# Expert tiles for half of the feed-forward chunks of a fused feed-forward, attention, feed-forward kernel

## Chip, cores and metric

One core of a Trainium2 chip. The metric is the device time of one execution in microseconds (us); the program is timed in several runs, and one more execution is recorded by the hardware profiler.

## The reference

x is 16 sequences of 256 tokens with 128 features, 4096 tokens in all, in float32. Three residual steps follow each other:

```
x = x + 0.5 * ffn(layernorm(x))
x = x + attention(layernorm(x))        # 16 heads of 64, causal
x = x + 0.5 * ffn(layernorm(x))        # the same weights
```

The feed-forward has 64 routed experts (128 to 64 to 128, SiLU gate) and one shared expert:

```
scores = sigmoid(x @ gate_w.T);  sc = scores + gate_bias
group_scores = top_k(sc in 8 groups of 8, 2).sum;   keep the best 4 groups
tidx = top_k(masked sc, 8);   tw = 2.5 * scores[tidx] / sum(scores[tidx])
y = sum over experts e:  w_dense[:, e] * ((silu(x @ wg[e]) * (x @ wu[e])) @ wd[e])
y = y + (silu(x @ sg) * (x @ su)) @ sd
```

Only 8 of the 64 weights w_dense[:, e] of a token are not zero.

## The kernel before

Tokens are cut into 8 chunks of 512 (CT = 4 tiles of 128). Both feed-forwards are one function, `ffn` (L382 on), with attention (L936 on) between them, each in a block of its own.

**Dense slots.** A chunk passes 33 slots: 32 pairs of experts, which fill the 128 rows of TensorE together, and the shared expert alone. In slot q TensorE computes gate and up of pair q (`up`, L491) and the down product of pair q - 3 (`down`, L510). Every token is multiplied with every expert. Gate and up weights, and the normalised tokens xT, are split in a high and a low float32r part, and `three` (L485 to L489) forms each product from three matmuls:

```
nc.tensor.matmul(bank[:, :], hi, rhs_hi, start=start, stop=False)                 # L487
nc.tensor.matmul(bank[:, :], lo, rhs_hi, start=False, stop=False)                 # L488
return nc.tensor.matmul(bank[:, :], hi, rhs_lo, start=False, stop=stop)           # L489
```

The down product (L521) is one float32 matmul of 512 columns into the bank `acc`, over all 33 slots of the chunk. ScalarE turns the gate into `hid` by SiLU (L592), VectorE multiplies it with up (`gated_product`, L648) and with the routing weights (`weighted_product`, L659). TensorE reports gate_done, up_done and down_done, one update each per slot. `hid` has three buffers (HIDS).

**Routing weights.** VectorE works out the mix of the next chunk in 25 route steps (`route`, two per slot from slot 14); TensorE turns it, ScalarE copies it to mixT, SyncE stores it to `mix_rows` in HBM (L363) and reads it back, spread over the partitions, as `mix_wide` (L789, L792): 8 groups of four slots per chunk, two transfers of 512 KB each, double-buffered.

**Turning.** A chunk also has transposes of the normalised tokens (L164), of the logits (L177), of the mix (L184) and of y (L528), and three matmuls for the logits (L170).

**Attention.** 64 steps, one for four heads of one sequence: q, k and v projections from split weights (L1024 to L1026, L1042 to L1044), scores (L1059) with the mask (L1063), 12 transposes of the probabilities (L1080), values (L1099), output (L1116). ScalarE does the exponentials (L1188, L1191), copies k (L1201) and the turned probabilities (L1210). VectorE copies q (L1255), v (L1263) and o (L1284), normalises (L1270, L1275) and takes the maxima (L1292, L1293). During its last steps the first chunk of the second feed-forward is routed.

GpSimd computes only constants and 1/sqrt of the variances (L348, L353). The order on each engine is written out by hand in its block; the loops over chunks run in `Fori` loops.

## Time and profile before

| | us |
|---|---|
| median of 3 runs (lowest, highest) | 1830.7 (1830.08, 1833.13) |
| the profiled execution | 1831.43 |
| its span, first to last instruction | 1829.7 |
| TensorE matmuls busy | 1781.7 (97%) |
| TensorE weight loads busy (beside the matmuls) | 1255.0 (69%) |
| VectorE busy | 1331.9 (73%) |
| ScalarE busy | 774.6 (42%) |
| GpSimd busy | 36.6 (2%) |

PE is TensorE's matmuls, PEld its weight loads, DVE is VectorE, ACT ScalarE, POOL GpSimd, SP SyncE; PEq, SPq are their instruction queues. Durations of matmuls overlap, since they are pipelined, so distances between starts say more than durations. A bracket at the end of a row tells how long the engine had been idle before it and what released it. The DMA share is that of the core's 16 DMA engines.

### The profile page before, as it was taken

To read this page: it belongs to the slowest core of one execution; us is meant where nothing else is said; L and a number is where in the kernel's file an instruction comes from. 1 tells how busy PE (TensorE), PEld (TensorE's weight loads), DVE (VectorE), ACT (ScalarE), POOL (GpSimd) and SP (SyncE) were. 2 spreads that over 40 slices of the span, in tenths; PEclk is the share of its full clock that TensorE was granted. 3 is DMA by queue.
4 is the path that set the end of the run, shared out by engine and by line. 5 is a ranking of instruction groups with operands and counts; after the bars stand their busy time and mean duration, and the time that the engine had idled before them with its cause. 6 is when DMAs were issued, how large, how long until landed. Compare 5 with 4: busy or idle time off the path is not lost.

```text
span 1829.7 us, 30208 instructions
## 1 busy us (share of the span) xinstructions
PE 1781.7 (97%) x9049; PEld 1255.0 (69%) x9049; DVE 1331.9 (73%) x3327; ACT 774.6 (42%) x1971; POOL 36.6 (2%) x84
## 2 busy tenths in 40 slices
PE   5899999999999999999999999879999999999999
PEld 3566666666666667777778777756666666666665
DVE  5777677676776678888888888767677676777765
ACT  3333323233232256767666666633323233232322
POOL 0000000000000000000000000000000000000000
PEclk8999999999999999999999999999999999999999
DMA  9954554455545500000000000034554455544553
GB/s 206 173 122 110 115 117 105 107 115 115 117 100 109 116 1 2 0 0 0 0 0 0 0 0 0 1 82 109 120 118 108 107 122 121 117 104 111 120 124 75
DMA packets 109530, 149.60 MB, mean 82 GB/s; under 512 B 30128, under 2 KB 43056, under 8 KB 109488
## 3 DMA queue, kind: packets, MB, share of 16 engines
q1 hardware_dynamic: 109488, 149.08, 36.9%
q8 instruction: 21, 0.34, 0.1%
q14 instruction: 21, 0.17, 0.0%
HBM read 144.87 MB, written 4.19 MB: 81 GB/s over the span
## 4 chain that ended last, share of the span: by engine, by line
PE 61%; DVE 2%; DMA 0%; issue 0%; ACT 0%; SPq 0%; POOLq 0%; POOL 0%; DVEq 0%
PE banks L521 12%; PE banks L489 7%; PE banks L487 7%; PE banks L488 7%; PE banks L1059 6%; PE banks L1099 5%; PE banks L1080 4%; PE banks L1116 3%; PE banks L1024 2%; PE banks L1063 2%; PE banks L1025 2%; PE banks L1026 2%; PE banks L1043 1%; PE banks L1044 1%; PE banks L1042 1%; DMA f_mix_wide<-mix_rows 0%
## 5 line engine op out<-in xcount | busy, mean ns | idle before, releaser
L592 ACT ACTIVATE f_hid<-banks 128x512 f32<-128x512 f32 x528 | 315.4, 597 | 835.9 <-PE banks L521 831.5
L648 DVE TENSOR_TENSOR f_hid<-banks,f_hid 128x512 f32<-128x512 f32 x528 | 363.9, 690 | 338.0 <-ACT f_hid L592 336.3
L521 PE MATMUL banks<-f_hid,wd 128*128 128x512 f32 x1056 | 540.7, 594 | 10.7 <-DVE f_hid L659 10.6
L487 PE MATMUL banks<-r_xT_hi,wg_hi 128*128 (+1 forms) x528 | 393.0, 744 | 2.4 <-PEq L951 2.4
L659 DVE TENSOR_TENSOR f_hid<-f_mix_wide,f_hid 128x512 f32<-128x512 f32 x512 | 352.9, 690 | 38.4 <-DMA f_mix_wide<-mix_rows 24.3
L521 PEld LDWEIGHTS banks<-f_hid,wd 128*128 128x128 f32 x1056 | 196.8, 188 | 67.6 <-DVE f_hid L659 13.1
L487 PE MATMUL banks<-r_xT_hi,wu_hi 128*128 (+1 forms) x528 | 209.9, 398 | 0.0
L489 PE MATMUL banks<-r_xT_lo,wu_hi 128*128 (+1 forms) x528 | 209.9, 398 | 0.0
L488 PE MATMUL banks<-r_xT_hi,wu_lo 128*128 (+1 forms) x528 | 208.8, 396 | 0.0
L489 PE MATMUL banks<-r_xT_lo,wg_hi 128*128 (+1 forms) x528 | 208.3, 394 | 0.0
L488 PE MATMUL banks<-r_xT_hi,wg_lo 128*128 (+1 forms) x528 | 207.3, 393 | 0.0
L487 PEld LDWEIGHTS banks<-r_xT_hi,wg_hi 128*128 128x128 f32 x528 | 100.6, 190 | 111.2 <-issue 110.2
L488 PEld LDWEIGHTS banks<-r_xT_hi,wg_lo 128*128 128x128 f32 x528 | 100.9, 191 | 108.2 <-issue 107.3
L1210 ACT COPY a_probT<-banks 128x512 f32<-128x512 f32 x192 | 106.3, 587 | 147.7 <-PE banks L1080 147.7
L1275 DVE TENSOR_SCALAR a_prob<-a_prob,a_inv 128x128 f32<-128x128 f32 (+1 forms) x512 | 129.0, 316 | 4.5
L1191 ACT ACTIVATE a_prob<-banks,a_bias 128x256 f32<-128x256 f32 x256 | 123.6, 483 | 0.0
L1059 PE MATMUL banks<-a_kT,a_qT 64*128 64x128 f32 (+1 forms) x1024 | 118.5, 350 | 0.3 <-issue 0.2
L489 PEld LDWEIGHTS banks<-r_xT_lo,wu_hi 128*128 128x128 f32 x528 | 99.2, 188 | 24.7
L489 PEld LDWEIGHTS banks<-r_xT_lo,wg_hi 128*128 128x128 f32 x528 | 99.6, 189 | 22.5
L487 PEld LDWEIGHTS banks<-r_xT_hi,wu_hi 128*128 128x128 f32 x528 | 99.6, 189 | 22.4 <-issue 0.4
L488 PEld LDWEIGHTS banks<-r_xT_hi,wu_lo 128*128 128x128 f32 x528 | 99.5, 188 | 22.6
L1080 PE MATMUL banks<-ident,a_prob 128*128 128x128 f32 x768 | 106.4, 275 | 1.1 <-DVE a_prob L1275 1.0
(153 smaller groups left out, 2155.4 us busy)
## 6 DMA issues: line engine op xcount, KB each, us to landing
f_mix_wide<-mix_rows SPq DMA_DIRECT2D x252, 512.0 KB, 6.5
landing<-in_L_ffn_We_gate SPq DMA_DIRECT2D x4, 512.0 KB, 7.1
landing<-in_L_ffn_We_up SPq DMA_DIRECT2D x4, 512.0 KB, 7.8
wd<-in_L_ffn_We_down SPq DMA_DIRECT2D x4, 512.0 KB, 6.8
mix_rows<-r_mixT SPq DMA_DIRECT2D x32, 64.0 KB, 2.1
out<-x_all SPq DMA_DIRECT2D x8, 256.0 KB, 6.7
f_mix_wide<-mix_rows SPq DMA_DIRECT2D x4, 384.0 KB, 5.4
f_mix_wide<-mix_rows SPq DMA_DIRECT2D x4, 128.0 KB, 3.0
```

Of the source, the lines that this page charges most:

```text
L487: nc.tensor.matmul(bank[:, :], hi, rhs_hi, start=start, stop=False)
L488: nc.tensor.matmul(bank[:, :], lo, rhs_hi, start=False, stop=False)
L489: return nc.tensor.matmul(bank[:, :], hi, rhs_lo, start=False, stop=stop)
L521: nc.tensor.matmul(acc[:, :], w["wd"][:, p * P:(p + 1) * P], hid[:, p % HIDS, :], start=(p == 0), stop=(p == PAIRS)).then_inc(down_done, 1)
L592: nc.scalar.activation(hid[:, p % HIDS, :], gate_bank[p % 3][:, :], ACT.Silu).then_inc(silu_done, 1)
L648: nc.vector.tensor_tensor(hid[:, p % HIDS, :], up_bank[p % 3][:, :], hid[:, p % HIDS, :], ALU.mult)\
L659: nc.vector.tensor_tensor(hid[:, p % HIDS, :], mix_wide[:, g % 2, p % SPREAD, :], hid[:, p % HIDS, :], ALU.mult).then_inc(weighted, 1)
L1059: nc.tensor.matmul(scores[pair][h][:, cols], qT[side_rows, i, pair, rows_q], kT[side_rows, i, pair, cols_k], start=(cols.start == 0), stop ...
L1080: mm = nc.tensor.transpose(bank[:, j * P:(j + 1) * P], prob[:, n * P:(n + 1) * P], w["ident"][:, :])
L1191: e = nc.scalar.activation(prob[:, o + P:o + NPB], scores[pair][h][:, P:NPB], ACT.Exp, bias=bias[:, i, pair, 1, h:h + 1], scale=HD ** -0.5 ...
L1210: nc.scalar.copy(probT[:, g * 4 * P:(g + 1) * 4 * P], turn_bank[g][:, :]).then_inc(probT_done, 1)
L1275: m = nc.vector.tensor_scalar(prob[:, a:b], prob[:, a:b], inv[:, i, pair, late, h:h + 1], None, ALU.mult)
```

## The change

Of the 8 chunks of each feed-forward four stay dense (0 to 3 in the first, 4 to 7 in the second) and four become sparse.

**Sparse chunks.** Their tokens are routed to a list: VectorE marks the eight experts of each token, counts per expert and lays the 16,384 (token, expert) rows out by expert, each expert's share rounded up to whole tiles of 128 rows (`plan`, `place`). GpSimd writes the normalised tokens by 128 indirect transfers, 128 rows of 512 bytes each, to `x_rows` in HBM (`dispatch`). The rows fill at most 191 tiles, taken by fours in QUADS_R = 48 **quads**; four more quads carry the shared expert. A quad: SyncE loads 4 tiles (256 KB), TensorE turns them, multiplies them with gate and up of the expert of each tile, turns the hidden rows, multiplies them with down; ScalarE and VectorE copy between, and SyncE stores 256 KB to `y_rows`. Which expert a tile belongs to is read at run time into registers of TensorE (`load_experts`). Four pipeline stages of successive quads stand in one step. Then GpSimd fetches the eight result rows of each token (`gather`, 128 more indirect transfers) and VectorE adds them with their weights (`add`), for the first feed-forward during attention (4 per step), for the second one between dense slots (8 per five slots, from slot 39). Before the first scatter `x_rows` (12.6 MB) is cleared by 12 transfers of 1 MB from ScalarE's queue, one every third slot from slot 16 (`clear_rows`). The first scatter begins at slot 57 of 132, the second in attention step 49 with 60 of its 128 transfers; the other 68 follow in the second feed-forward, whose quads stand behind its first dense chunk.

**Dense slots.** Gate, up and down are one float32 matmul each; the split weights and their making are gone. Only the up product reports (`pair_done`), and the down product once per chunk (`chunk_done`); `hid` has four buffers. VectorE takes three route steps per slot.

**Attention.** Fully written out. The copies of q and v move to ScalarE, the output product behind the v projection, and the sparse chunks of the second feed-forward and its first dense one are normalised and routed here.

The diff replaces most of the file; its core (line numbers are of the new file):

```diff
@@ dense slot, TensorE (L764 on)
-            def up(c, p):
...
-                if p >= 3 or not first:
-                    pe.wait_ge(silu_done, SLOTS * c + p - 2)
...
-                three(g, "wg", p, xh, xl).then_inc(gate_done, 1)
-                if p >= 3 or not first:
-                    pe.wait_ge(gated, SLOTS * c + p - 2)
...
-                three(u, "wu", p, xh, xl).then_inc(up_done, 1)
...
-            def down(c, p):
-                if p == PAIRS:
-                    pe.wait_ge(gated, SLOTS * (c + 1))
-                else:
-                    pe.wait_ge(weighted, PAIRS * c + p + 1)
...
-                nc.tensor.matmul(acc[:, :], w["wd"][:, p * P:(p + 1) * P], hid[:, p % HIDS, :],
-                                 start=(p == 0), stop=(p == PAIRS)).then_inc(down_done, 1)
+        def up(g):
+            c, p = divmod(g, SLOTS)
+            x = d.xT[:, c % 2, :]
...
+            experts = slice(2 * p, 2 * p + rows // F)
+            if g >= 3:
+                pe.wait_ge(silu_done, g - 2)
...
+            nc.tensor.matmul(gate_bank[g % 3][0:rows, :], w["gu"][:, 0, experts, :].rearrange("p e f -> p (e f)"), x,
+                             start=True, stop=True)
+            if g >= 3:
+                pe.wait_ge(gated, g - 2)
+            nc.tensor.matmul(up_bank[g % 3][0:rows, :], w["gu"][:, 1, experts, :].rearrange("p e f -> p (e f)"), x,
+                             start=True, stop=True).then_inc(pair_done, 1)
...
+        def down(g):
+            c, p = divmod(g, SLOTS)
+            if p == PAIRS:
+                pe.wait_ge(gated, g + 1)
+            else:
+                pe.wait_ge(weighted, PAIRS * c + p + 1)
...
+            rows = F if p == PAIRS else P
+            mm = nc.tensor.matmul(acc[:, :], w["wd"][0:rows, 2 * p, :], d.hid[0:rows, g % HIDS, :],
+                                  start=(p == 0), stop=(p == PAIRS))
+            if p == PAIRS:
+                mm.then_inc(chunk_done, 1)
@@ quads, TensorE (L561 on)
+        def load_experts(j):
+            if j < SPARSE:
+                expert[j] = [E] * CT
+                return
+            i = j - SPARSE
+            if i == 0:
+                pe.wait_ge(r.plan_step, PLAN_STEPS - 1)
+            _, expert[j] = nc.values_load_multi_w_load_instructions(
+                b.ids[i:i + 1, :], engines=PE_ONLY, min_val=0, max_val=E,
+                skip_runtime_bounds_check_because="the number of 64 experts that end at or before a tile")
...
+        def gate_up(j):
+            load_experts(j)
+            e = expert[j]
+            pe.wait_ge(xT_copied, j + 1)
+            if j >= 2:
+                pe.wait_ge(hid_done, j - 1)
+            for t in range(CT):
+                wt = w["gu"][:, :, e[t], :] if j < SPARSE else \
+                    w["gu"][:, :, bass.ds(e[t], 1), :].rearrange("p k a f -> p k (a f)")
+                mm = nc.tensor.matmul(B[j % 2][:, t * P:(t + 1) * P], q.xqT[:, j % 2, t * P:(t + 1) * P], wt,
+                                      start=True, stop=True)
+            mm.then_inc(gu_done, 1)
...
+        def step(j):
+            if ok(j):
+                turn(j)
+            if ok(j - 1):
+                gate_up(j - 1)
+            if ok(j - 2):
+                turn_hid(j - 2)
+            if ok(j - 3):
+                down(j - 3)
@@ quads, SyncE (L692 on)
+        def load(i):
+            if i == 0:
+                sp.wait_ge(r.scattered, 16 * TOPK * CT * SPARSE)
+            if i >= 3:
+                sp.wait_ge(turned, SPARSE + i - 2)
+            sp.dma_start(q.xq[:, i % 3, :, :], rows(x_rows, i)).then_inc(loaded[i % 3], 16)
+        def store(i):
+            sp.wait_ge(y_read, SPARSE + i + 1)
+            sp.dma_start(rows(y_rows, i), q.yq[:, i % YBUFS, :, :]).then_inc(y_stored[i % YBUFS], 16)
@@ GpSimd
+        def dispatch(i):
+            tile, half = divmod(i, 2)
+            k, t = divmod(tile, CT)
+            if t == 0 and half == 0:
+                pool.wait_ge(idx_done, k + 1)
+            for j in HALVES[half]:
+                nc.gpsimd.indirect_dma_start(
+                    x_rows[:, :], bass.IndirectOffsetOnAxis(ap=b.idx[:, f, CT * k + t, j:j + 1], axis=0),
+                    b.xk[:, k, t, :], None).then_inc(scattered, 16)
...
+        def gather(t, js=range(TOPK)):
+            if t >= GBUFS and js[0] == 0:
+                pool.wait_ge(added, added_before + TOPK * (t - GBUFS + 1))
+            for j in js:
+                nc.gpsimd.indirect_dma_start(
+                    g_buf[:, t % GBUFS, j, :], None, y_rows[:, :],
+                    bass.IndirectOffsetOnAxis(ap=b.idx[:, f, t, j:j + 1], axis=0)).then_inc(gathered[t % GBUFS], 16)
@@ the added rows, VectorE
+                nc.vector.scalar_tensor_tensor(x, g_buf[:, t % GBUFS, j, :], b.w8[:, f, t, j:j + 1], x,
+                                               ALU.mult, ALU.add).then_inc(added, 1)
@@ attention, ScalarE (L1346 on)
+            def slot(c, k, last):
+                soft = k >= 1 and (k - 1 < STEPS or not last)
+                if soft:
+                    exps(c, k - 1)
+                if k < STEPS or not last:
+                    copy_q(c, k)
+                    copy_k(c, k)
+                if k % QUADS == 1 and k >= LEAD_A:
+                    copy_y(c, k)
+                if soft:
+                    copy_probT(c, k - 1)
+                if k < STEPS or not last:
+                    copy_v(c, k)
```

On TensorE's queue a dense slot in the middle of a chunk of the first feed-forward was this (f_hid are the hidden rows, r_xT the normalised tokens):

```order
L487 MATMUL banks<-r_xT_hi,wg_hi 128x512 [waits f1_silu_done]
L488 MATMUL banks<-r_xT_hi,wg_lo 128x512
L489 MATMUL banks<-r_xT_lo,wg_hi 128x512
L487 MATMUL banks<-r_xT_hi,wu_hi 128x512 [waits f1_gated]
L488 MATMUL banks<-r_xT_hi,wu_lo 128x512
L489 MATMUL banks<-r_xT_lo,wu_hi 128x512
L521 MATMUL banks<-f_hid,wd 128x512 [waits f1_weighted]
```

and a slot of the changed kernel, followed by the next slot and a routed quad step (f1q_xq the loaded rows, f1q_hidT the turned hidden rows, r_ids the expert numbers), are these on the same queue:

```order
L778 MATMUL banks<-r_xT_d,gu 128x512 [waits f1d_silu_done]
L782 MATMUL banks<-r_xT_d,gu 128x512 [waits f1d_gated]
L794 MATMUL banks<-f1_hid,wd 128x512 [waits f1d_weighted]
```

```order
L556 MATMUL banks<-ident,f1q_xq 128x128 [waits f1q_xT_copied,f1q_loaded1]
L556 MATMUL banks<-ident,f1q_xq 128x128 x3
L568 TENSOR_LOAD r_ids
L581 ISA [waits f1q_hid_done,f1q_xT_copied]
L581 MATMUL banks<-gu,f1q_xqT 128x128
L581 ISA
L581 MATMUL banks<-gu,f1q_xqT 128x128
L581 ISA
L581 MATMUL banks<-gu,f1q_xqT 128x128
L581 ISA
L581 MATMUL banks<-gu,f1q_xqT 128x128
L591 MATMUL banks<-ident,f1q_hidq 128x128 [waits f1q_hT_odd_copied,f1q_hT_even_copied,f1q_hid_done]
```

Seven matmuls became three. In the quad step two transposes of hidden rows and four down products, each behind its own address instruction, follow the last row; the register load stands between the transposes and the gate products.

On ScalarE's queue an attention step of the changed kernel runs from the q copy to the v copy like this (L1312 and L1320 stood on VectorE's):

```order
L1312 COPY a_qT<-banks 128x512 [waits a_proj_done,a_scores_done]
L1328 COPY a_kT<-banks 128x512 [waits a_proj_done,a_scores_done]
L1337 COPY a_probT<-banks 128x512 [waits a_o_done,a_prob_turned]
L1337 COPY a_probT<-banks 128x512 [waits a_prob_turned] x2
L1320 COPY a_v<-banks 128x512 [waits a_proj_done,a_o_done]
```

The v copy stands behind the last copy of the turned probabilities, and the next step's exponentials behind it.

## Rows read from the trace of the kernel before

**Rows 1.** Busy time by stretch: us, busy us (x instructions), clock, DMA share, GB/s
```profile
0.00:652.80 652.80, 624.55 (x2259) 416.91 (x2259) 450.58 (x999) 209.04 (x338) 13.65 (x38) 0.99 0.55 121
652.80:1211.90 559.10, 545.08 (x4555) 427.97 (x4555) 456.50 (x1408) 373.18 (x1318) 14.55 (x32) 0.99 0.00 0
1211.90:1829.70 617.80, 612.12 (x2235) 410.09 (x2235) 424.84 (x920) 192.38 (x315) 8.44 (x14) 1.00 0.51 114
```
**Rows 2.** Timeline of TensorE, one dense slot: start us, us, engine line
```profile
400.76 0.79 PE L487 MATMUL banks<-r_xT_hi,wg_hi 128*128 x1
401.39 0.39 PE L488 MATMUL banks<-r_xT_hi,wg_lo 128*128 x1
401.61 0.39 PE L489 MATMUL banks<-r_xT_lo,wg_hi 128*128 x1
...
403.00 0.79 PE L487 MATMUL banks<-r_xT_hi,wg_hi 128*128 x1
```
**Rows 3.** Timeline, the last four down products
```profile
1821.28 3.62 PE L521 MATMUL banks<-f_hid,wd 128*128 128x512 f32 x8
```
**Rows 4.** Timeline, turning of y in two successive chunks
```profile
1298.93 0.60 PE L528 MATMUL banks<-ident,r_yT 128*128 128x128 f32 x4
...
1375.57 0.60 PE L528 MATMUL banks<-ident,r_yT 128*128 128x128 f32 x4
```
**Rows 5.** Timeline of TensorE and its weight loads, parts of one attention step
```profile
802.54 0.74 PEld L1116 LDWEIGHTS banks<-a_oT,po 128*128 128x128 f32 x4
...
802.66 1.02 PE L1116 MATMUL banks<-a_oT,po 128*128 128x256 f32 x4
...
803.64 0.28 PE L1043 MATMUL banks<-pv_lo,n_xT_hi 128*128 128x256 f32 x1
803.75 0.28 PE L1044 MATMUL banks<-pv_hi,n_xT_lo 128*128 128x256 f32 x1
...
805.84 1.04 PE L1080 MATMUL banks<-ident,a_prob 128*128 128x128 f32 x8
806.81 0.93 PE L1059 MATMUL banks<-a_kT,a_qT 64*128 64x128 f32 x8
...
807.99 1.52 PE L1099 MATMUL banks<-a_probT,a_v 128*64 128x256 f32 x16
```
**Rows 6.** Busy time in two stretches of the first feed-forward, columns as in rows 1
```profile
10.00:20.00 10.00, 8.31 (x23) 6.30 (x24) 7.07 (x21) 6.07 (x8) 0.00 (x0) 1.00 1.28 226
...
300.00:400.00 100.00, 100.00 (x366) 67.26 (x365) 73.44 (x178) 30.83 (x52) 1.21 (x2) 1.00 0.51 112
```
**Rows 7.** The page's DMA issues, the mix store: count, size, us to landing
```profile
mix_rows<-r_mixT SPq DMA_DIRECT2D x32, 64.0 KB, 2.1
```
**Rows 8.** Timeline of ScalarE, two copies of turned probabilities
```profile
806.48 1.07 ACT L1210 COPY a_probT<-banks 128x512 f32<-128x512 f32 x2 [1.03 <-PE banks L1080]
```
**Rows 9.** Timeline, first matmuls of attention and of the second feed-forward
```profile
652.84 0.35 PE L1024 MATMUL banks<-n_xT_hi,pq_hi 128*128 128x256 f32 x1 [1.05 <-PEq L399]
...
1211.94 0.47 PE L487 MATMUL banks<-r_xT_hi,wg_hi 128*128 128x512 f32 x1 [2.36 <-PEq L951]
```
**Rows 10.** Waits of ScalarE in 700 to 1100: total us, times, longest
```profile
ACT a_probT L1210 <- PE banks L1080: 109.2, 95, 1.4
```
**Rows 11.** Waits of VectorE in 0 to 110: total us, times, longest
```profile
DVE f_hid L659 <- DMA f_mix_wide<-mix_rows: 19.5, 5, 6.4
```
**Rows 12.** Timeline of VectorE in a routed dense slot
```profile
401.00 0.68 DVE L659 TENSOR_TENSOR f_hid<-f_mix_wide,f_hid 128x512 f32<-128x512 f32 x1
...
401.60 0.42 DVE L325 TENSOR_TENSOR r_chosen<-r_chosen,r_score 128x256 f32<-128x256 f32 x1
...
402.05 0.69 DVE L648 TENSOR_TENSOR f_hid<-banks,f_hid 128x512 f32<-128x512 f32 x1
```
**Rows 13.** Timeline of SyncE's queue at the start, two issues
```profile
1.32 0.59 SPq L830 DMA_DIRECT2D f_gw_raw<-in_L_ffn_gate_w  x1
...
3.05 2.37 SPq L810 DMA_DIRECT2D landing<-in_L_ffn_We_up  x1
```
**Rows 14.** Timeline of GpSimd, one layer norm
```profile
1151.48 1.01 POOL L353 TENSOR_TENSOR r_rstd<-r_veps,minus_half 128x4 f32<-128x4 f32 x1
```

More of the change, by code:

```diff
@@ L36 @@
 NG = 8
+TOPK = 8
 TOPK_GROUPS = 4
@@ new lines, with routes_of @@
+TILES = (TOPK * SPARSE * CHUNK - E) // P + E
+QUADS_R = -(-TILES // CT)
+ROWS = QUADS_R * CHUNK
+QUADS_ALL = SPARSE + QUADS_R
+PAD = E // 2
+YBUFS, STORE_LAG, GBUFS = 3, 6, 3
+HALVES = (range(0, TOPK // 2), range(TOPK // 2, TOPK))
+DENSE_STEPS = 25
+SPARSE_STEPS = 23
+PLAN_STEPS = 12
+PLACE_STEPS = 4
+W_STEPS = 3
+WEIGH_STEPS = W_STEPS * CT + 5
+@dataclass(frozen=True)
+class Route:
+    n: int
+    front: int
+    chunk: int
+    dense: int
+    sparse: int
+def routes_of(kinds, by_row=0):
+    out, d, s = [], 0, 0
+    for n, (chunk, is_dense) in enumerate(kinds):
+        out.append(Route(n, n - by_row, chunk, d if is_dense else -1, -1 if is_dense else s))
+        d, s = d + is_dense, s + (not is_dense)
+    return out
@@ L931, in row_norm, with attention @@
     return parts
-def attention(nc, w, x_all, banks, psum, rows, ahead):
+A_ROUTE, A_COUNT, A_PLAN, A_RANK, A_DISPATCH = 14, 44, 45, 48, 49
+A_HEAD, A_MIX = 47, 55
+ADD_LAG = 3
+def attention(nc, w, x_all, banks, psum, rows, b, mix_rows, y_rows, first, second, gathered, added):
     TB = SEQ // P
@@ L942, in attention @@
     QUADS = H // 4
-    STEPS = 2 * QUADS
+    STEPS = NB * QUADS
+    PER_CHUNK = CHUNK // SEQ
+    FRONTS = [4 * n for n in range(SPARSE * PER_CHUNK)] + [32, 37]
+    chunk_of = [q.chunk for q in FIRST if q.sparse >= 0]
+    later, head = [q for q in SECOND if q.sparse >= 0], SECOND[SPARSE]
     NPB = P + SEQ
@@ L1111, in output @@
                         pe.wait_ge(x_updated, b)
-                    if not (last and k == QUADS):
+                    if b + 1 < NB:
                         pe.wait_ge(xT_lo_done, b + 2)
@@ L1159, in slot @@
                     turn_prob(c, k - 1, 2, live)
-                if k % QUADS == 1 and not last:
+                if k % QUADS == 1 and k // QUADS + 1 < NB:
                     turn_xn(c, k)
@@ L1351, in _ @@
+            for k in range(STEPS):
+                if k < 2 * SPARSE * CT:
+                    gather(k // 2, HALVES[k % 2])
+                if k >= A_DISPATCH:
+                    dispatch(k - A_DISPATCH)
+                if front_row(k, 6) is not None:
+                    front_rstd(front_row(k, 6))
+                if moments_row(k) is not None:
+                    rstd_of(moments_row(k))
         @block.sync
         def _(sp):
-            ahead.on_sync(sp)(0)
+            second.on_sync(sp, mix_rows)(head)
@@ L1390, in macaron @@
+        gathered = [ctx.enter_context(nc.semaphore(f"gathered{i}")) for i in range(GBUFS)]
+        added = ctx.enter_context(nc.semaphore("added"))
         banks = ctx.enter_context(nc.psum_tensor("banks", [P, 8 * 512], F32))
         psum = [banks[:, i * 512:(i + 1) * 512] for i in range(8)]
-        b = router_buffers(ctx, nc)
-        first, second = (router(ctx, nc, tag, w, x_all, mix_rows, b) for tag in ("r1_", "r2_"))
-        rows = row_norm(ctx, nc, w, x_all)
-        ffn(nc, "f1_", w, x_all, psum, mix_rows, b, first, rows=rows, load=(x_v, dr))
```

1829 lines of the change are left out of this document (1181 added, 648 removed).

## The prediction

> **What bounds the kernel now.** I read the busy time by stretch first, for the stages and their clock; then TensorE in time order inside a stage; then the other engines and the queues at the same places. The kernel has three stages, first feed-forward, attention, second feed-forward, of 652.8, 559.1 and 617.8 us [rows 1]. TensorE is at work in nearly all of each, at a granted clock of 0.99 to 1.00, which is the 2.4 GHz level. VectorE has 451, 456 and 425 us of work in them, ScalarE at most 373. So TensorE's work sets the time, and what an edit is worth is how much of that work it takes out or adds, plus any new wait that ends last.
>
> One slot of a feed-forward (two experts for 512 tokens) lasts 2.24 us: the first gate product starts at 400.76 and the next slot's at 403.00 [rows 2]. Six split products stand some 0.23 us apart (401.39 and 401.61 are two of them); the down product, one full-precision matmul made of two records, takes the rest, about 0.85 us. The records' own durations overlap, so I go by starts. The four down products at the end confirm the size: 8 records in 3.62 us, 0.45 each with the tail [rows 3]. A whole chunk lasts 76.64 us from one turning of y to the next [rows 4]: 33 slots of 2.24, and 2.7 us for turning, logits and mix.
>
> **Dense slots.** Four of the eight chunks of each feed-forward keep the slots, so 528 become 264. The slot itself changes: the split weights are gone, and gate, up and down are each one full-precision product of 512 columns. Three times 0.85 is 2.55, three times 0.9 is 2.7; I take 2.58, near the back-to-back starts. A dense slot thus gets longer by 0.34 us. Removed 528 x 2.24 = 1183 us, put in 264 x 2.58 = 681 us: -502. Of the 14 routed chunks inside the feed-forwards 10 are left, 4 x 2.7 = -11. That gate and up now report once together, and down only once per chunk, I cost at nothing: ScalarE starts SiLU 0.85 us later, but the down product comes three slots after, and a fourth hid buffer covers the reuse.
>
> **Quads.** Each feed-forward gets 52 steps (4 with the shared expert, 48 of four sorted tiles). One step on TensorE is 4 transposes, 4 gate/up products of 128 columns, 2 transposes and 4 down products. A transpose takes 0.12 us by its neighbours' starts (8 of them from 805.84 to 806.81), and it too is one weight load and 128 columns [rows 5]. A full-precision product is two such halves. The output product of attention has four halves of 256 columns in the 0.86 us from 802.66 to the start of the split product before 803.64, 0.215 each, so 128 columns stream in 0.107, under the 0.12. That gives (4 + 2 + 2 x 4 + 2 x 4) x 0.12 = 2.64, say 2.7 us. The step also loads four expert numbers into registers on TensorE's queue, and then computes each address. The trace has no such load. Below it costs nothing: a loop branch and register work stand in every chunk now and TensorE is at work in all 100 us of a stretch [rows 6], so its queue runs ahead. Above, it costs a memory round trip of 2.1 us, as the 64 KB mix store takes [rows 7], less the 0.5 us of transposes queued ahead. I take 0.3, near the low end, because the down products and transposes of the same step stand ahead of the load and need nothing late. So 3.0 us a step (2.7 to 4.3), and 104 x 3.0 = +312. The Trainium skill (DMA: Bandwidth & Descriptors, Latency and other measured facts) gives a register load a floor of about 600 ns. By that and a queue that does not run ahead at all a step would be 2.8 to 3.3 us and the sum -21 to +31 us from mine; no run here shows it yet.
>
> The other engines fit in a step. ScalarE has about 1.3 us (two 512-column copies take 1.07 together [rows 8], here one and two smaller), VectorE 1.5 us. SyncE moves 256 KB in and 256 KB out; at the 226 GB/s seen while weights in 256 and 512 byte pieces came in [rows 6] that is 2.3 us, so DMA is close behind and comes next if TensorE is faster than I think.
>
> **Joins.** Dense drains, quads fill, the last y rows must land before the gathers: a new block restarts TensorE's queue in 1.05 and 2.36 us today [rows 9], and the quads' pipeline of four steps fills and empties once; I take 12 us per feed-forward, +24 (12 to 40).
>
> **Attention.** The q and v copies leave VectorE for ScalarE. ScalarE now waits 109 us for transposes in 400 us, 2.3 us a step of 8.3 [rows 10], and takes 1.1 more. But the v copy comes after the last probT copy, which ends at 807.55 [rows 8]; the values product behind it starts at 807.99 today [rows 5] and needs the v copy, so it moves to about 808.2: 0.2 us x 64 = +13 (0 to 37). TensorE gets ten more turnings, logits, counts and ranks: +9. VectorE receives 128 weighted additions of 128 columns and the routing, about 2.6 us in a full step (4 x 0.3 and 4 x 0.35, from 0.45 for 256 columns [rows 12]). The two copies that left, 0.69 each by rows of their size [rows 12], give 1.4, and VectorE is idle in (559 - 456) / 64 = 1.6 us of a step [rows 1]: it fits, with little to spare. Sum +22 (5 to 60).
>
> **First chunks.** The clears of the row buffer add 12.6 MB to mix tiles that already made VectorE wait 19.5 us in the first 110 us [rows 11]; +10 (0 to 35). In routed slots VectorE has two 0.60 products and three 0.45 route steps [rows 12], 2.55 of 2.58 us, and LayerNorm spills over: +6 (0 to 20).
>
> **Sum.** 1829.7 - 502 - 11 + 312 + 24 + 22 + 10 + 6 = 1690.7, and 1.7 us outside the span (the profiled execution took 1831.4, the median is 1830.7): **1692 us**.
>
> **GpSimd.** It issues 128 indirect transfers per scatter or gather, 512 in all, 128 rows each. No row shows one. SyncE's plain issues take 0.6 us, those into full rings up to 2.4, GpSimd's own power on four columns 1.01 [rows 13, 14]; I take 1.3 us, and for that T all are hidden: the first scatter has some 229 us (slot 57 to the end of the first quads, T up to 1.8), the second has 68 transfers left in about 99 us (1.46), a gather of 8 has five slots, 12.9 us (1.6), an attention step takes 4 (2.1).
>
> **Rivals.**
> - GpSimd becomes the bound, slower than before. The excess is 128(T - 1.8) + 68(T - 1.46) + 128(T - 1.6); it reaches 139 us, and the present time, at T = 2.07; at 2.1 the kernel takes 1838. For it: VectorE's weighted product reads two SBUF tiles and runs 0.68 of every 2.58 us [rows 12], and if an issue has to wait out one, 1.3 becomes 2.0. Against it the trace has nothing, since GpSimd hardly works in it; and the operations of that kind fill a quarter of a slot. The Trainium skill (SBUF - State Buffer, SBUF: two separate sides) states such a lock between a VectorE operation with two SBUF inputs and a GpSimd operation that reads SBUF; no run here shows it. 10%.
> - Loads do not overlap products: each of the 22 halves costs the 0.19 us of a load record (4 in 0.74 [rows 5]) and not 0.12, a step 4.5 us, 1848 us (2%). Split products of 256 columns 0.12 us apart, each with its load [rows 5], speak against it. Or the register load is wholly exposed, 1827 us (5%).
> - DMA sets the step: 512 KB at half the seen rate is 4.7 us, 1869 us. 3%.
> - It goes better than that: queue ahead of everything, quads 2.7, v copy and clears free: 1692 - 31 - 13 - 16 = 1632. 10%.
> - My case, 70%, 1640 to 1760.
>
> **The numbers.** What a measurement can tell from no change is 0.2%, 3.7 us. Faster has my case, the good one and half of the exposed load, 83%; same the other half, 2%; slower the three that remain, 15%. The range takes the good case in and reaches up to 1.1 us more per quad step: 1630 to 1805.
>
> **What would show it.** Right: starts of gate products 2.58 us apart; quad transposes 3.0 us apart; attention steps some 0.3 us longer than now; first indirect gathers 1.3 us apart on GpSimd, and no wait for scattered rows ahead of the first routed quad. Wrong: TensorE idle behind its own queue in each quad step; VectorE waiting on gathered rows; a second stage over 600 us; slots of the first chunk stretched by mix tiles for much over 20 us.

## The result and the profile after

The changed kernel takes **2058.2 us** (median of 4 runs, 2055.3 to 2061.2) against 1831.9 for the one before: 1.124 times as long (95% interval 1.121 to 1.126). Forecast were 1692 us, and a range up to 1805. The page of the changed kernel (busy us, share of the span, instructions; then tenths in 40 slices):

```profile
span 2053.6 us, 26930 instructions
PE 1659.6 (81%) x8683; PEld 1054.5 (51%) x8683; DVE 1197.8 (58%) x3446; ACT 779.5 (38%) x2105; POOL 549.6 (27%) x607
PE   5899792399999777777678997639738999898899
POOL 1000657600000433323230002360570000646430
PEclk9999995699999888888889998869969999999899
```

TensorE has 1660 us of work and stands for 394. It was at work in nearly all of each stage before [rows 1]. The slices in which it falls (the fifth, seventh and eighth, the 14th to 21st, the 25th to 27th, the 29th and 30th) are slices in which GpSimd is at work. Stretches of it, cut by time, say the same more finely. Columns: TensorE, weight loads, VectorE, ScalarE, GpSimd (busy us, instructions), granted clock, DMA share, GB/s.

```profile
208.00:412.00 204.00, 115.89 (x249) 48.29 (x248) 83.66 (x210) 29.37 (x47) 129.48 (x130) 0.77 0.33 87
275.00:300.00 25.00, 25.00 (x69) 11.77 (x68) 21.38 (x48) 9.26 (x13) 19.31 (x20) 1.00 0.51 129
300.00:325.00 25.00, 12.39 (x22) 4.27 (x20) 6.38 (x25) 1.22 (x3) 19.21 (x20) 0.69 0.36 95
325.00:350.00 25.00, 4.99 (x6) 1.80 (x6) 5.38 (x12) 1.17 (x2) 19.20 (x20) 0.57 0.28 76
1350.00:1375.00 25.00, 0.00 (x0) 0.00 (x0) 0.52 (x2) 1.72 (x8) 18.90 (x21) 0.51 0.16 52
```

From 275 to 300 us all is well beside 20 indirect transfers of GpSimd. From 300 on the transfers go on at the same pace and the three compute engines all but stop, with no engine busy in their place and the DMA engines two thirds idle. From 1350 to 1375, in attention, which needs no data from memory but the gathers, already done by then, TensorE executes nothing at all. What ends it shows in the timelines (start us, us, engine, line, what; in brackets the idle time before and what ended it). ScalarE, then VectorE, then TensorE:

```profile
310.21 0.60 ACT L822 ACTIVATE f_hid<-banks 128x512 f32<-128x512 f32 x1 [9.41 <-remote]
324.98 0.60 ACT L822 ACTIVATE f_hid<-banks 128x512 f32<-128x512 f32 x1 [14.17 <-remote]
341.77 0.60 ACT L822 ACTIVATE f_hid<-banks 128x512 f32<-128x512 f32 x1 [16.19 <-remote]
357.87 0.60 ACT L822 ACTIVATE f_hid<-banks 128x512 f32<-128x512 f32 x1 [15.50 <-remote]
```
```profile
325.60 0.69 DVE L844 TENSOR_TENSOR f_hid<-banks,f_hid 128x512 f32<-128x512 f32 x1 [11.00 <-issue]
```
```profile
301.22 1.02 PE L778 MATMUL banks<-r_xT_d,gu 128*128 128x512 f32 x2
302.08 1.02 PE L782 MATMUL banks<-r_xT_d,gu 128*128 128x512 f32 x2
302.94 1.02 PE L794 MATMUL banks<-f_hid,wd 128*128 128x512 f32 x2
303.80 1.02 PE L778 MATMUL banks<-r_xT_d,gu 128*128 128x512 f32 x2
304.65 1.02 PE L782 MATMUL banks<-r_xT_d,gu 128*128 128x512 f32 x2
...
310.86 2.07 PE L778 MATMUL banks<-r_xT_d,gu 128*128 128x512 f32 x2 [4.33 <-ACT f_hid L822]
312.73 1.92 PE L782 MATMUL banks<-r_xT_d,gu 128*128 128x512 f32 x2
...
325.62 2.08 PE L778 MATMUL banks<-r_xT_d,gu 128*128 128x512 f32 x2 [8.38 <-issue]
```

A SiLU (L822) waits for one thing, the semaphore that the up product (L782) raises, and TensorE may be three slots ahead of it. The slot that starts at 310.86 needs the SiLU of three slots before, at 310.21; so the SiLU at 324.98 belongs to the slot of 301.22, that at 341.77 to 303.80, that at 357.87 to 310.86. Their up products ended at 303.1, 305.7 and 314.6 (the profile models a matmul's end, but the down product started no more than 0.5 us behind each of them): the updates were seen **22, 36 and 43 us late**, one of them about every 16 us. "remote" is the profile's word for a releaser that it cannot name: the update came long after its matmul. In the other directions nothing is late. VectorE (325.60) starts as ScalarE ends, and TensorE (325.62) beside it. The hold in attention is of the same kind: VectorE waits for TensorE's values product, and goes on 2 us after the last transfer of that run.

```profile
1375.60 0.96 POOL L467 DMA_INDIRECT x_rows<-r_xk,r_idx  x1 [0.31 <-issue]
```
```profile
1378.95 0.69 DVE L1447 COPY a_oT<-banks 128x512 f32<-128x512 f32 x1 [28.40 <-remote]
1381.82 0.59 ACT L1312 COPY a_qT<-banks 128x512 f32<-128x512 f32 x1 [29.52 <-PE banks L1164]
```

The waits, summed, put it in one list (who waited for whom, us in all, times, longest). The long ones of ScalarE and VectorE end with TensorE's updates or an unnamed releaser; those of TensorE follow from them:

```profile
ACT f_hid L822 <- remote: 196.1, 20, 16.2
DVE f_hid L844 <- issue: 178.7, 32, 21.0
PE banks L1162 <- DVE a_oT L1447: 161.8, 40, 31.2
DVE a_oT L1447 <- remote: 102.2, 10, 28.4
ACT a_qT L1312 <- remote: 51.0, 9, 9.9
DVE f_hid L857 <- DMA f_mix_wide<-mix_rows: 26.4, 5, 8.8
```

The waits of ScalarE and VectorE that end with an unnamed releaser are none in the kernel before and 428 us in 63 waits in the changed one. The experiments use this sum as the sign of the hold.

### The profile page after: what moved, and what is told of

It is laid out like the page before. It is cut to its first block and busy times, and to the rows that moved or that the text cites. A ratio compares the mean times of both kernels' runs of the same rounds, so it can differ in the third digit from the quotient of the medians.

```text
span 2053.6 us, 26930 instructions
## 1 busy us (share of the span) xinstructions
PE 1659.6 (81%) x8683; PEld 1054.5 (51%) x8683; DVE 1197.8 (58%) x3446; ACT 779.5 (38%) x2105; POOL 549.6 (27%) x607
## 3 DMA queue, kind: packets, MB, share of 16 engines
q0 software_dynamic: 16384, 33.59, 5.9%
## 5 line engine op out<-in xcount | busy, mean ns | idle before, releaser
L822 ACT ACTIVATE f_hid<-banks 128x512 f32<-128x512 f32 (+1 forms) x264 | 156.8, 597 | 683.1 <-PE banks L782 432.5
L844 DVE TENSOR_TENSOR f_hid<-banks,f_hid 128x512 f32<-128x512 f32 (+1 forms) x264 | 181.7, 688 | 352.6 <-issue 178.7
L778 PE MATMUL banks<-r_xT_d,gu 128*128 128x512 f32 x528 | 293.1, 638 | 114.6 <-issue 86.3
L467 POOL DMA_INDIRECT x_rows<-r_xk,r_idx x256 | 252.3, 985 | 189.5 <-issue 79.5
L794 PE MATMUL banks<-f_hid,wd 128*128 128x512 f32 x528 | 282.3, 619 | 22.4 <-DVE f_hid L857 11.4
L782 PE MATMUL banks<-r_xT_d,gu 128*128 128x512 f32 x528 | 286.7, 626 | 0.0
L778 PEld LDWEIGHTS banks<-r_xT_d,gu 128*128 128x128 f32 x528 | 100.1, 201 | 241.2 <-issue 202.5
L857 DVE TENSOR_TENSOR f_hid<-f_mix_wide,f_hid 128x512 f32<-128x512 f32 x256 | 175.6, 686 | 28.9 <-DMA f_mix_wide<-mix_rows 26.4
L501 POOL DMA_INDIRECT f_g<-y_rows,r_idx x128 | 128.2, 1002 | 209.4 <-DMA y_rows<-f2q_yq 132.3
L782 PEld LDWEIGHTS banks<-r_xT_d,gu 128*128 128x128 f32 x528 | 105.5, 200 | 139.1 <-issue 133.1
L501 POOL DMA_INDIRECT a_g<-y_rows,r_idx x128 | 124.7, 975 | 141.4 <-POOLq L1582 104.5
L1299 ACT ACTIVATE a_prob<-banks,a_bias 128x128 f32<-128x128 f32 x256 | 98.3, 384 | 75.5 <-DVE a_bias L1459 59.1
```

The source lines that it names most:

```text
L467: nc.gpsimd.indirect_dma_start(x_rows[:, :], bass.IndirectOffsetOnAxis(ap=b.idx[:, f, CT * k + t, j:j + 1], axis=0), b.xk[:, k, t, :], Non ...
L501: nc.gpsimd.indirect_dma_start(g_buf[:, t % GBUFS, j, :], None, y_rows[:, :], bass.IndirectOffsetOnAxis(ap=b.idx[:, f, t, j:j + 1], axis=0 ...
L778: nc.tensor.matmul(gate_bank[g % 3][0:rows, :], w["gu"][:, 0, experts, :].rearrange("p e f -> p (e f)"), x, start=True, stop=True)
L782: nc.tensor.matmul(up_bank[g % 3][0:rows, :], w["gu"][:, 1, experts, :].rearrange("p e f -> p (e f)"), x, start=True, stop=True).then_inc( ...
L794: mm = nc.tensor.matmul(acc[:, :], w["wd"][0:rows, 2 * p, :], d.hid[0:rows, g % HIDS, :], start=(p == 0), stop=(p == PAIRS))
L822: nc.scalar.activation(d.hid[0:rows, g % HIDS, :], gate_bank[g % 3][0:rows, :], ACT.Silu)\
```

## Experiments

**Theory A**: while GpSimd issues transfers back to back, TensorE's semaphore updates reach their waiters late. **Theory B**: the other terms of my sum were too low (quads, clears, a fuller attention step). Every time below stands beside 1830 to 1833 us for the kernel before. e7, e9, e11 and e14 are medians of four executions, the others are single ones; those of one kernel lay up to 14 us apart (e7), in the others within 6.

**1. No transfers at all, and plain ones.** e1 leaves GpSimd's 512 transfers out, and with them SyncE's wait for the scattered rows; one fill per tile stands for the eight gathers. e2 changes only the kind of the transfers. So e1's sorted rows stay zero and e2's land in a fixed order: both compute something else than the reference, with the same instructions on the other engines.

```
-  nc.gpsimd.indirect_dma_start(x_rows, idx..., b.xk[:, k, t, :])
+  nc.gpsimd.dma_start(x_rows[n:n + P, :], b.xk[:, k, t, :])      # plain; the gathers likewise
```

> All 512 indirect transfers of GpSimd are left out (the rows of the sorted tiles stay zero, the gathered buffers are filled with zeros by one memset a tile), everything else stays. Theory A (while GpSimd issues its transfers back to back, TensorE's semaphore updates reach ScalarE and VectorE 10 to 16 us late): the stalls go, about 75 us in the first stage, 150 to 200 in attention, 80 in the second, and the time falls to 1660 to 1760 us. Theory B (the other work was under-priced: quads, the clears, the fuller attention step): the time stays above 1900 us.

> Each of the 512 indirect transfers is replaced by a plain one of the same 128 rows of 512 bytes, issued by GpSimd at the same places (rows land in a fixed order, so the output is another). If what hurts is any run of GpSimd transfers back to back, the time stays within 40 us of 2055. If it is the indirect kind (index reads, scattered rows), it falls below 1800 us.

Measured: **1689.8** without transfers, **1690.5** with plain ones. Theory B falls, and so does "any transfer of GpSimd's": 512 plain transfers with as many rows and bytes cost 0.7 us, which is no difference between single executions. Neither kernel has a wait with an unnamed releaser. They even run denser, 81 in a row at 0.53 us each, against 1.26 for an indirect one (0.96 and 0.30 between). The timeline of GpSimd with plain transfers, and the indirect ones of the changed kernel:

```profile
259.86 42.91 POOL L468 DMA_DIRECT2D x_rows<-r_xk  x81
```
```profile
310.33 0.96 POOL L467 DMA_INDIRECT x_rows<-r_xk,r_idx  x1 [0.30 <-issue]
311.60 1.10 POOL L467 DMA_INDIRECT x_rows<-r_xk,r_idx  x1 [0.31 <-issue]
```

The stages can be read off the same matmuls in every run: the first quad with sorted rows in the first feed-forward, the first and last output product of attention, the first sorted quad of the second feed-forward (lines of the tiles' views, us of the first to the last).

```profile
L556 PE MATMUL banks<-ident,f1q_xq x192: 272/273/330, 517.4 to 648.9; 128*128 128x128 f32 x192
L1232 PE MATMUL banks<-a_oT,po x256: 377/379/634, 689.4 to 1447.5; 128*128 128x256 f32 x128
L556 PE MATMUL banks<-ident,f2q_xq x192: 272/273/332, 1608.7 to 1741.6; 128*128 128x128 f32 x192
```
```profile
L554 PE MATMUL banks<-ident,f1q_xq x192: 272/273/330, 412.7 to 544.2; 128*128 128x128 f32 x192
L1230 PE MATMUL banks<-a_oT,po x256: 377/378/634, 577.6 to 1180.4; 128*128 128x256 f32 x128
L554 PE MATMUL banks<-ident,f2q_xq x192: 272/273/332, 1280.9 to 1413.8; 128*128 128x128 f32 x192
```

The first three are the changed kernel, the last three the one with plain transfers. So the indirect transfers cost 105 us in the first scatter (517.4 against 412.7), 155 in attention (758.1 against 602.8), 61 in the rest of the second scatter (161.2 against 100.5) and 37 in the last gathers: 444.9 to the end against 407.9. With the 7 us at attention's start that is the whole 365.

In attention the runs are shorter: between 660 and 1074 us GpSimd issues its gathers in runs of 4 and 12; the second scatter then stands in runs of 12, 16 and 32.

**2. Rests, and a slower pace.**

```
+  pool.wait_ge(dn.weighted, weighted_by(58 + int(2.5 * i)))   # e3: before each four of the first scatter
+  nc.gpsimd.memset(b.idle[:, 0:1024], 0.0)  ...               # e4: and a wait for it, behind each transfer
```

> GpSimd rests between groups of four transfers: it waits for VectorE's weighted product of slot 58 + 2.5 i in the first stage, of every second slot in the rest of the second scatter, for one score maximum per attention step, and twice per five slots for the last gathers. Theory A with bursts (the delay builds up over some 15 to 20 transfers in a row): four in a row do no harm, 1690 to 1790 us, second scatter (little room for rests) being what is left. If each transfer costs its share wherever it stands: 2000 us and more.

> Behind every transfer GpSimd fills a scratch of 1024 columns and waits for that, so its transfers come some 2.2 to 2.4 us apart in place of 1.26, without a rest anywhere. Theory A by rate: TensorE's updates come at once again, and what is left is GpSimd's own lateness, 128 x 2.3 against 229 us in the first scatter, 68 x 2.3 against 99 in the second, 128 x 2.3 against 257 in the last gathers: +65, +57 and +40 on about 1690, so 1800 to 1900 us. If the number of transfers counts and not their rate: 2150 us or more.

Measured: **1775.7** with rests, **2004.3** with the padding. Rests alone turn 1.124 into 0.97 of the kernel before. They are fewer than the edit says, since a rest is a wait for a slot, and a late GpSimd passes it without resting: in attention the kernel has its fours, in the first scatter 4 to 12 in a row and 15 at the end, but the second scatter holds two runs of 20, and the last gathers begin with 32 in a row. Its waits with an unnamed releaser (75 us in 23) lie there but for 18 us:

| kernel | time | waits with an unnamed releaser: us, times, longest |
|---|---|---|
| changed | 2058 | 428, 63, 28.4 |
| e3, rests | 1776 | 75, 23, 10.0 |
| e4, 2.25 us apart | 2004 | none |
| e13, 1.52 us apart | 1729 | 3, 2, 2.5 |
| e9, even rests | 1716 | 26, 8, 6.7 |
| e2, plain transfers | 1691 | none |

The padded kernel misses its range by 104 us, with its transfers 2.25 us apart as expected. There is no wait with an unnamed releaser left in it, but GpSimd is late everywhere: beside plain transfers the first sorted quad comes 98 us later (510.5; TensorE waits 70 us for the scattered rows there), attention takes 66 more (668.4 between its output products), the stretch to the second's first sorted quad 62, and the last part 86 (493.6). I had priced 65, 57 and 40 in the feed-forwards and nothing in attention. So at 2.25 us the holds are gone, at the price of a GpSimd that sets the end.

**3. Which transfers, and what of them.**

```
# e5: the changed kernel with the gathers of e2; its scatters stay indirect
-  ap=b.idx[:, f, CT * k + t, j:j + 1] ... b.xk[:, k, t, :]
+  ap=b.idx[0:32, f, CT * k + t, j:j + 1] ... b.xk[0:32, k, t, :]    # e6; the gathers likewise
```

> As the changed kernel, without rests, but the 256 gathers are plain transfers of 128 rows and only the 256 scatters stay indirect. If the indirect kind does harm in both directions, the parts with scatters keep their losses (105 us before the first sorted quad, the 28 us hold at the end of attention, 60 before the second's quads) and the parts with gathers lose nothing (some 125 us in attention and 37 at the end go): 1855 to 1900 us. If only writes to scattered rows hurt, the same; if only gathers hurt, 1750 or less.

> Indirect transfers as in the changed kernel, as many and in the same places, but of 32 of the 128 rows each (the other rows are left out of scatter and gather). If TensorE's updates are held by something that each row costs (an address made for each row, a descriptor written), the holds all but vanish: 1690 to 1740 us. If each transfer costs its share whatever its size (its issue, its 16 completions), the time stays at 1950 us or more, unless the issues themselves come further apart.

Measured: **1916.7** with plain gathers, **2072.2** with a quarter of the rows (both again compute something else than the reference). With plain gathers the last part is free of loss (409.6 us to the end), and the scatters keep theirs (first sorted quad at 516.7): both directions do harm. The time is 17 us above my range, since the scatters inside attention cost more than the 28 us that I had put to them: 668.2 us between its output products, 65 above plain transfers. The other 90 us of attention's loss (758.1 against 668.2) belong to its gathers, though they stand in runs of 4 and 12. And a transfer of 32 rows does the same harm as one of 128 (issued 0.87 + 0.30 us apart). In the stretch of the first scatter the kernel with 32 rows moves 57 GB/s in place of 87 and still stands:

```profile
208.00:412.00 204.00, 118.38 (x244) 48.27 (x242) 82.60 (x211) 27.41 (x43) 119.91 (x130) 0.76 0.25 57
```

So neither the bytes nor the number of rows sets the hold; the indirect kind does, at this pace. What in that kind does it (the index it reads, how its addresses are made) was not tried.

**4. One update per slot, or three.** The third part of the change, undone by itself.

```
+  nc.tensor.matmul(gate_bank...).then_inc(gate_done, 1)     # and ScalarE waits for gate_done, not pair_done
+  mm.then_inc(down_done, 1)                                  # each down product, and SiLU waits for it
```

> The kernel with rests, with the three updates per dense slot of the kernel before put back (gate, up and down each report; SiLU waits for gate and for the down product four slots earlier, the gate product on VectorE for up too). Theory A (each update of TensorE takes its turn behind GpSimd's address work, one after the other): where transfers run, a slot waits for more updates, so some 20 to 80 us above the 1775 of one update. If the number of updates does not matter: within 8 us of it.

> Plain transfers everywhere, three updates per dense slot. With no indirect transfer in it an update costs nothing: within 5 us of the 1690.5 of one update, or a few us less, since SiLU can start after gate alone. If updates cost TensorE time by themselves: 264 x 2 x 0.03 to 0.1 = 15 to 50 us more.

Measured: **1771.9** (1766.4 to 1780.2) with rests, **1682.7** with plain transfers. Three updates are not slower: 8 us faster with plain transfers (single executions), where SiLU starts behind the gate product in 264 slots, and 4 us with rests, which is within the spread. The range of 20 to 80 us that I gave theory A was wrong. Both kernels with rests keep holds in their long runs (waits with an unnamed releaser of 75 us in e3 and 94 in e7), and three updates in a slot didn't make the time longer by what passes one by one would cost; why not is open. Whether one update is worth it without rests, where updates pass one in 16 us, was not tried.

**5. How to rest.**

```
+  rest(n)                                      # e9: before every transfer: 1.6 per dense slot (2 in the
+  pool.wait_ge(normed, 2 * k)                  #     second scatter), two and two in an attention step
                                                # e11: e9 with the three updates of e7
+  weighted_by(58 + int(2.5 * (i - i % 4)))     # e10: e3 with sixteen in a row in the first
                                                #      scatter (i % 8 in e12: 32)
+  nc.gpsimd.memset(b.idle[:, 0:192], 0.0)      # e13: and a wait for it, behind each transfer
                                                # e14: e11 with five per attention step, 1.72 per slot
```

> Rests as before, but spread: GpSimd waits before every transfer, not before every four (1.6 transfers per dense slot in the first scatter and the last gathers, two per slot in the second scatter, two and two in an attention step). The holds grow with the transfers in a row, so by theory A runs of one or two leave nothing to wait for outside the second scatter: 1715 to 1750 us. If the mean rate is what counts, nothing changes: 1765 to 1785 us.

> The kernel with rests, but in the first scatter sixteen transfers in a row and then a rest of about 6 us, at the same mean rate; the rest unchanged. The changed kernel took some 16 to 20 transfers from the start of a run to its first long hold. If the run's length is what counts and its threshold lies there, a hold of a few us at the end of some runs: 1780 to 1800 us (first sorted quad at 430 to 445 us, 423 with fours). If only the mean rate counts: 1775, first sorted quad at 423 us. If short runs already cost in proportion: above 1820.

> The evenly spread transfers with the three updates per dense slot of the kernel before. With plain transfers three updates were 8 us faster (SiLU starts after the gate product), with rests by fours 4 us, within the spread. So 3 to 8 us below the even kernel, 1710 to 1745 us. If each update has to queue behind GpSimd, 5 us or more above it.

> The kernel with rests by fours, but in the first scatter 32 transfers in a row (40 us) and then some 11 us of rest, the same mean rate as with runs of 4 and 16, which both reached the first sorted quad at 423 to 424 us. If a run's length counts (the holds began after 16 to 20 transfers of a run in the changed kernel), each of the four runs ends in one or two holds of 5 to 16 us: first sorted quad at 445 to 480 us, total 1785 to 1835. If the mean rate alone counts: 424 us and 1764 to 1776.

> The changed kernel without rests, with a small fill of 192 columns behind every transfer, so that they come about 1.5 us apart in place of 1.26, without an end. If there is a backlog that grows by what each transfer needs beyond the pitch, and the need is no more than the 1.6 us of the kernels with rests: no holds or few, and GpSimd's lateness is small (128 x 1.5 against 229, 68 x 1.5 against 99), 1695 to 1760 us. If a run without rest is what hurts, whatever its pitch: holds as before, above 1950 us.

> The even kernel with three updates, with five transfers of the second scatter per attention step in place of four, so that 53 in place of 68 are left for the 33 slots behind (1.65 per slot in place of 2), and 1.72 per slot in the first scatter. The 25 us of the second stage's start between the even kernel and the one with plain transfers should halve, and the first sorted quad comes 3 to 6 us sooner: 1695 to 1710 us; 1714 or more if five per step hold attention up.

Measured: e9 **1716.3** (0.937 of the kernel before, 0.9355 to 0.9381), e10 **1764.2**, e11 **1714.1** (0.935, 0.9337 to 0.9364), e12 **1812.3**, e13 **1729.2**, e14 **1716.6**. The same 204 us of the first scatter, with 125 to 130 of its transfers and LayerNorm's few operations in them (e12 has only three of its four runs inside), for e3 (fours), e10 (sixteens), e12 (thirty-twos) and e13 (no rest, 1.52 us apart), in this order:

```profile
208.00:412.00 204.00, 198.00 (x501) 87.49 (x499) 147.07 (x316) 53.04 (x86) 129.17 (x127) 1.00 0.51 125
```
```profile
208.00:412.00 204.00, 199.43 (x504) 87.94 (x502) 147.00 (x321) 53.39 (x87) 130.75 (x126) 1.00 0.51 126
```
```profile
208.00:412.00 204.00, 158.72 (x361) 66.62 (x360) 116.28 (x269) 40.46 (x66) 97.18 (x98) 0.89 0.41 103
```
```profile
208.00:412.00 204.00, 199.12 (x507) 88.32 (x507) 148.19 (x321) 54.79 (x90) 166.57 (x253) 1.00 0.50 127
```

249 matmul records in the changed kernel, 501 to 507 with fours, sixteens or the small pause, 361 with thirty-twos: at the same mean rate runs of 16 cost nearly nothing and runs of 32 do. The step between them isn't sharp. e10 has short holds too: at the end of its first run (ScalarE waits 5.6 us, at 229.8, where 2 are usual), of its fourth (5.1 us, at 312.4), and of the fifth and sixth, which a rest of 0.75 us hardly parts (3.8 and 4.3 us, at 361.1 and 366.1); the slots still catch up, and the first sorted quad comes 0.8 us after that of e3 (423.4). e12's comes at 475.9, against 424.2 with sixteens. ScalarE's waits in the first run of e12, which starts at 209.8, have the old picture, and end with the run:

```profile
221.86 0.60 ACT L822 ACTIVATE f_hid<-banks 128x512 f32<-128x512 f32 x1 [1.35 <-issue]
232.06 0.59 ACT L822 ACTIVATE f_hid<-banks 64x512 f32<-64x512 f32 x1 [7.02 <-remote]
241.88 0.60 ACT L822 ACTIVATE f_hid<-banks 128x512 f32<-128x512 f32 x1 [9.24 <-remote]
255.19 1.09 ACT L822 ACTIVATE f_hid<-banks 128x512 f32<-128x512 f32 x2 [12.71 <-remote]
```

And the small pause alone is enough: 0.27 us of fill, 1.52 in place of 1.26 us from transfer to transfer, GpSimd at work without end, and 1729 us in place of 2058.

```profile
301.85 0.96 POOL L468 DMA_INDIRECT x_rows<-r_xk,r_idx  x1 [0.28 <-POOL r_idle L471]
302.81 0.27 POOL L471 MEMSET r_idle<- 128x192 f32 x1
303.36 0.97 POOL L468 DMA_INDIRECT x_rows<-r_xk,r_idx  x1 [0.28 <-POOL r_idle L471]
```

So both guesses hold together, for the slots: the hold comes in a run that is long **and** has its transfers 1.26 us apart, and it is gone at 1.52. Where between the two it begins, and whether the time or the wait for the fill does it, was not tried.

Attention is more tender than the slots. Fours cost it 21 to 35 us (633.3, 624.2, 627.3 and 637.4 us between its first and last output product in e3, e10, e12 and e7; 602.8 with plain transfers), two and two nothing (603.2 in e9), the small pause 11 (613.7 in e13). Of its waits with an unnamed releaser in e3 none is longer than 1.8 us, so this is not the long hold of the slots; what makes it up was not followed. Even rests give way too where GpSimd is late: e9 has a run of 30 in the second scatter. Three updates gain 2 us with them (e11 against e9). e14, with five per step in its last 15 steps, gets 10 us back in the second stage's first chunk (101.5 in place of 111.3) and 3 at the first sorted quad, and loses 26 in attention (629.7). It came out 7 us above its range, by the rival that its expectation names (five per step hold attention up), and e11 and e14 can't be told apart. The best kernel measured that computes the reference's result is e11, even rests and three updates, 118 us below the kernel before and 31 above plain transfers with three updates (e8).

## Why the prediction was wrong

**The step that failed** is in the part on GpSimd: "I take 1.3 us, and for that T all are hidden". T was right: 1.26. "Hidden" I took to mean in time, before the rows are needed, and in time they were: VectorE waited 1.1 us in all for gathered rows. The rival that I built on GpSimd's lateness (a bound from T = 2.07 on, by a lock between VectorE's two-input products and GpSimd) asked for late rows too, and fell with T. That lock, for which I had named the Trainium skill (SBUF — State Buffer, SBUF: two separate sides), does show here, but small. Of the 128 issues of the first scatter 77 run beside no VectorE product with both inputs in SBUF, and none of them takes over 0.97 us; of the 51 beside one, 16 take over 1.1, the longest 1.44, and the mean is 1.06. One such case, at the start of the second feed-forward (GpSimd's issue ends 0.84 us after VectorE's product):

```profile
1458.90 0.69 DVE L857 TENSOR_TENSOR f_hid<-f_mix_wide,f_hid 128x512 f32<-128x512 f32 x1 [2.62 <-DMA f_mix_wide<-mix_rows]
1459.01 1.42 POOL L467 DMA_INDIRECT x_rows<-r_xk,r_idx  x1 [0.30 <-issue]
```

In e13, where no engine stands, the mean beside such a product is 1.08. So the trace agrees that an issue can have to wait out a product, and the rival's price was too high: 0.1 us an issue in the mean, not 0.7. It isn't the hold either: during a hold VectorE stands, and most issues take 0.96.

What I didn't ask is what a run of transfers does to engines that neither wait for its data nor share its queue. My words for the third part of the change, that gate and up "now report once together" and down once per chunk, "I cost at nothing", looked at the number of updates and at ScalarE's start, not at what carries an update. No row of before could show the hold, since GpSimd issued no transfer there. But the change's own words, issues without rests, named the run, and a long run of a kind of transfer that no row shows was the place to put the slow rival, with the whole of GpSimd's 512 x 1.26 = 645 us as its bound.

**The rest of the sum**, read in the kernel without transfers, whose 1689.8 is 2 us from the 1692: closer than its terms are.
- Dense slots: gate products at 301.22 and 303.80, **2.58** apart, as taken; -502 stands. One update per slot in place of three costs 2 to 8 us (e9 against e11, e2 against e8), not nothing, and is no saving.
- Quads: 517.4 to 648.9 from the first of 48 steps to the last is **2.80** a step, not 3.0: 104 x 0.2 = 21 us too dear. TensorE is busy 25.00 of 25 us in them, so the load of expert numbers costs nothing that shows, and the rivals on it, on weight loads and on DMA fall (0.68 share, 190 GB/s).
- Attention: 540.0 us between its first and last output product before, 602.8 with plain transfers: **+63**, not +22, just over my upper 60; a step is 1.0 us longer, not 0.3. TensorE's busy time there grew by 20 us (530.1 to 550.4), and it now waits 48.6 us for VectorE's copy of the values' product (the row below). "It fits, with little to spare" counted VectorE's 1.6 us of idle time per step as free; my reading, not tested by a run, is that they were the slack of a chain.
- By stage, from first matmul to first matmul as in [rows 1], with plain transfers: the first feed-forward takes 557.1 us, 96 less than before, attention 625.3, 66 more, the second feed-forward 506.4, 111 less. My terms give 67 less, 22 more and 94 less. So the feed-forwards were 46 us too dear, 21 of them the quads, and attention 44 too cheap: that the sum came out is luck. Of the other 25 us only a part is traced: TensorE restarts at attention 5.6 us after the last quad and at the second feed-forward after 0.8, where I had 12 each for the joins, and VectorE's wait for the mix tiles is 22.3 us in the first 110 against 19.5 before, where I had +10 for the clears.

TensorE's waits for that copy, in attention of the kernel with plain transfers:

```profile
PE banks L1160 <- DVE a_oT L1445: 48.6, 30, 3.4
```

Two slips of the working change nothing: with its own terms the excess reaches 139 us at T = 2.08, not 2.07, and an attention step before was 8.6 us, not 8.3.

**What I had asked of the profile**: slots 2.58 apart came true, indirect issues 1.3 apart too, quads were 2.8 apart, attention steps were 1.0 us longer in place of 0.3. Of the signs against me one came, a second stage over 600 us (790 in the changed kernel, 625 with plain transfers), and one that I had not listed, ScalarE waiting 10 to 16 us for a product long done.

## What to carry to other kernels

Cost a queue of GpSimd's transfers not only by when its data are needed, but as a run: how long, how dense, and who must hear from TensorE meanwhile. A pause of a quarter of a microsecond per transfer was worth 329 us of 2058 here, and a wait that paces them by another engine's progress 342; never letting more than 16 stand in a row came out nearly as well in the slots of the first scatter. Such a wait paces only while GpSimd isn't late: look in the trace for the runs that are left. And where a sum agrees with the time, check its terms by stage before believing them: here some 40 us too little in attention met 40 too much in the feed-forwards.

## What the runs showed of the hardware

- While indirect transfers of GpSimd follow each other 1.26 us apart, TensorE's semaphore updates are seen late, in the dense slots from about the 12th to the 20th transfer of a run on: in one run 22 to 43 us late, one passing about each 16 us, until some 2 to 9 us after the run's end. Updates of ScalarE and VectorE are not. 1.52 us apart there was no such hold in 512 transfers (no wait with an unnamed releaser over 2.5 us), nor with plain transfers 0.53 us apart.
- An indirect transfer occupies GpSimd for 0.96 us with 128 rows and 0.87 with 32, and 0.30 lies between two; a plain one takes 0.53 in all. The 0.96 becomes up to 1.44 (first scatter) only beside a VectorE product with both inputs in SBUF. In the first scatters of e3, e9, e10 and e13 too every issue over 1.1 us runs beside one, most up to 1.5, one 2.28.
- TensorE's clock follows: 0.51 to 0.57 of full speed, the 1.2 GHz level, in stretches of 25 us in which it stands for most or all of the time, and 0.90 in the mean; the first matmuls after a hold take 2.07 us for 1.02.
- Not settled: what in the chip the updates wait for. The trace shows who is late and how the pace and the kind of transfer bear on it, not the path. That VectorE's and ScalarE's updates pass is read from timelines, not tried by an experiment of its own. Attention's losses with short runs (90 us with gathers in runs of 4 and 12, 21 to 35 with fours) are measured, not explained.
